# Two Swin blocks on one core: the bias of q and k moved from a matmul of its own into a constant channel of the normalised tile

## The reference, cut to what matters

```python
xn  = (x - mean(x)) * rsqrt(var(x) + 1e-5) * gamma + beta      # over the 192 channels
xs  = roll(xn, (-4, -4))                                       # windows of 8 x 8 = 64 tokens
qkv = xw @ w_qkv + b_qkv                                       # 192 -> 3 * 192, 12 heads of 16
...
x   = x + softmax(q @ k.T / 4 [+ bias + mask]) @ v @ w_proj + b_proj
x   = x + gelu(layernorm(x) @ w_fc1 + b_fc1) @ w_fc2 + b_fc2   # 192 -> 768 -> 192
```

## Time and profile before

| what | value |
|---|---|
| median of the runs, lowest, highest | 4314.11, 4303.97, 4317.73 us |
| the profiled execution, time and span | 4314.22 and 4312.3 us |
| TensorE clock granted, mean | 0.999 |
| PE matmul busy | 4027.5 us, 93% |
| PE weight load busy | 2912.2 us, 68% |
| VectorE (DVE) busy | 3364.9 us, 78% |
| ScalarE (ACT) busy | 2709.6 us, 63% |
| GpSimd (POOL) busy | 3062.7 us, 71% |
| DMA traffic | 420.50 MB, mean 98 GB/s |

### The profile page before, as it was taken

The page is one execution under the profiler, slowest core; times in us unless marked ns, Lnnn a source line. Parts: engine busy times, 40 slices in busy tenths (PEclk is TensorE's granted clock), DMA queues, the critical chain, the costliest instruction groups (busy, mean ns, idle before and its releaser), DMA issues. The chain is left out here.

```text
span 4312.3 us, 175439 instructions
## 1 busy us (share of the span) xinstructions
PE 4027.5 (93%) x66384; PEld 2912.2 (68%) x66384; DVE 3364.9 (78%) x9085; ACT 2709.6 (63%) x5921; POOL 3062.7 (71%) x6257
## 2 busy tenths in 40 slices
PE   4999999999999999999999999999999999999998
PEld 2666667667766666776676677667667766766665
DVE  6887777778778777787777778787777778777785
ACT  1666666666666666666666666666666666666665
POOL 4777777777777777777777777777777777777664
PEclk9999999999999999999999999999999999999999
DMA  4655556556565655555555555556555655565553
GB/s 98 104 96 100 98 95 99 102 95 99 104 98 97 100 102 92 103 100 96 98 100 98 97 99 102 97 97 101 102 91 101 100 97 98 100 101 96 90 95 61
DMA packets 1544449, 420.50 MB, mean 98 GB/s; under 512 B 1441334, under 2 KB 1542074, under 8 KB 1543612
## 3 DMA queue, kind: packets, MB, share of 16 engines
q1 hardware_dynamic: 1543612, 409.29, 54.9%
HBM read 31.56 MB, written 25.17 MB: 13 GB/s over the span
## 5 line engine op out<-in xcount | busy, mean ns | idle before, releaser
L573 PE MATMUL ps_s<-xh,w_fc 128*128 128x512 f16 x3840 | 909.7, 380 | 60.7 <-ACT stage L687 47.6
L941 DVE TENSOR_TENSOR hid<-scaled,hid 128x512 f16<-128x512 f32 x768 | 597.9, 779 | 449.7 <-POOL hid L1109 430.7
L1047 POOL TENSOR_TENSOR rstd<-vare,half 128x2 f32<-128x2 f32 x520 | 361.2, 695 | 801.5 <-DVE vare L881 801.5
L586 PE MATMUL bank<-w_fc,hid 128*128 128x192 f16 x9216 | 847.7, 246 | 77.7 <-DVE hid L941 71.9
L586 PEld LDWEIGHTS bank<-w_fc,hid 128*128 128x128 f16 x9216 | 764.6, 98 | 156.7 <-DVE v_blk L897 80.6
L573 PEld LDWEIGHTS ps_s<-xh,w_fc 128*128 128x128 f16 x3840 | 335.3, 97 | 621.0 <-ACT scaled L701 217.5
L1109 POOL TENSOR_SCALAR hid<-scaled 128x512 f16<-128x512 f32 x768 | 609.4, 794 | 182.8 <-ACT scaled L701 182.2
L701 ACT ACTIVATE scaled<-ps_s,b_fc 128x512 f32<-128x512 f32 x768 | 529.3, 690 | 308.9 <-DVE hid L941 306.8
L693 ACT ACTIVATE pt<-ps_t 128x768 f16<-128x768 f32 x512 | 415.3, 811 | 324.0 <-PE ps_t L530 316.8
L666 ACT ACTIVATE xs<-xn 128x192 f16<-128x192 f32 x512 | 184.6, 361 | 579.0 <-POOL xn L1053 579.0
L449 PE MATMUL bank<-w_qkv,xh 128*128 128x384 f16 x2560 | 500.9, 326 | 6.2 <-DMA xh<-xs 3.6
(11 more groups left out here) (113 smaller groups left out, 7341.9 us busy)
## 6 DMA issues: line engine op xcount, KB each, us to landing
x_img<-in_x_dram SPq DMA_DIRECT2D x256, 96.0 KB, 2.2
out_dram<-y_img SPq DMA_DIRECT2D x256, 96.0 KB, 1.9
xh<-xs SPq DMA_TRANSPOSE x520, 2.8
qkt<-qk SPq DMA_TRANSPOSE x512, 4.0
ot<-os SPq DMA_TRANSPOSE x512, 2.3
stage<-in_L_conv_fc_w_dram SPq DMA_DIRECT2D x2, 384.0 KB, 4.3
stage<-in_L_conv_w_fc_dram SPq DMA_DIRECT2D x2, 384.0 KB, 4.0
stage<-in_L_conv_qkv_w_dram SPq DMA_DIRECT2D x2, 288.0 KB
```

What stands on the lines that cost most here:

```text
L573: last = mm(ps_s[:, u % 2, :].rearrange("p (a t) -> p a t", a=GROUP), w_fc1[layer][:, part, m * 128:(m + 1) * 128], xh[:, p % 2 * GROUP:(p ...
L586: mm(bank[:, 0:C], hid16[:, hs, m, tok], w_fc2[layer][:, ws, m, :], start=(m == 0 and i == 0), stop=False)
L941: v.tensor_tensor(hid16[:, 1, m, :], hid[:, u % 2, :], hid16[:, 0, m, :], ALU.subtract)\
```

## The change

The bias matmul of `qk_product` goes. In its place the normalised tile's last channel (191) is the constant one in the high part and zero in the remainder, written once at the start. Since z sums to zero, z of channel 191 is minus the sum of the others; so the last weight row is subtracted from all rows (its own becomes zero), and that freed row of `w_qkv` gets the bias: its high part in the row of the high weights, its remainder in the row of the low weights. The columns of v keep a zero there.

In the steady state `normalise` for norm 1 and `norm1_lo` now write 191 channels. In the setup each layer gets two more loads before its first weight is ready (`w_last`, the last weight row on all 128 partitions, and `gain_last`), five more VectorE operations in `make_weight`, one copy less, and two small DMAs which write the bias into `w_qkv`, for which TensorE waits before the first slot. `rel` and `rel_t` are laid over `x_mid`, which is unused at that time.

```diff
-        b_qk = [sb(f"b_qk{l}", [128, 2 * C], F16) for l in range(LAYERS)]
+        qk_bias = sb("qk_bias", [1, LAYERS, 2, 2 * C], F16)
+        w_last = sb("w_last", [128, 3 * C], F32)
+        gain_last = sb("gain_last", [128, LAYERS], F32)
...
+                        last_row = L["wqkv"][C - 1:C, :]
+                        sp.dma_start(w_last[:, :], bass.AP(tensor=last_row.tensor, offset=last_row.offset,
+                                                           ap=[[0, 128], [1, 3 * C]])).then_inc(w_in[j], 16)
+                        last_gain = column(L["g1"], C - 1, 1)
+                        sp.dma_start(gain_last[:, l:l + 1], bass.AP(tensor=last_gain.tensor, offset=last_gain.offset,
+                                                                    ap=[[0, 128], [1, 1]])).then_inc(w_in[j], 16)
...
+                    if k == 3:
+                        for part in range(2):
+                            sp.dma_start(w_qkv[l][CB - 1:CB, 3 * part + 1, 0:2 * C], qk_bias[:, l, part, :])\
+                                .then_inc(bias_in, 16)
...
-        W_DMAS = [9, 4, 5, 1]
+        W_DMAS = [11, 4, 5, 1]
...
             pe.wait_ge(made, 1 + 4 * LAYERS)
+            pe.wait_ge(bias_in, 16 * 2 * LAYERS)
...
-                    contract(ps_qk[:, 0:2 * C], w_qkv[layer], xh[:, n % AHEAD, 0], 0, 2 * C, b_qk[layer][:, :])\
+                    contract(ps_qk[:, 0:2 * C], w_qkv[layer], xh[:, n % AHEAD, 0], 0, 2 * C)\
                         .then_inc(S["qk_mm"], 1)
...
-                v.memset(b_qk[l][:, :], 0.0)
...
+            v.memset(xs[:, :, 0, 0, C - 1:C].rearrange("p r c -> p (r c)"), 1.0)
+            v.memset(xs[:, :, 0, 1, C - 1:C].rearrange("p r c -> p (r c)"), 0.0)
...
+                if last is not None:
+                    for c0, c1, s in ((0, q_cols, WSCALE * QSCALE), (q_cols, n, WSCALE)):
+                        link(v.tensor_scalar(w_last[:, c0:c1], w_last[:, c0:c1], last, s, ALU.mult, ALU.mult))
+                    for rows in range(3):
+                        link(v.tensor_tensor(scaled[:, rows, 0:n], scaled[:, rows, 0:n], w_last[:, 0:n], ALU.subtract))
...
-                link(v.tensor_copy(row16[:, :], row[:, 0:2 * C]))
-                link(v.tensor_copy(b_qk[l][0:1, :], row16[:, :]))
-                link(v.tensor_tensor(b_qk[l][32:33, :], row[:, 0:2 * C], row16[:, :], ALU.subtract))
+                link(v.tensor_copy(qk_bias[:, l, 0, :], row[:, 0:2 * C]))
+                link(v.tensor_tensor(qk_bias[:, l, 1, :], row[:, 0:2 * C], qk_bias[:, l, 0, :], ALU.subtract))
...
-                    g_.tensor_scalar(dst, stream(n, which), nmean[:, r, which:which + 1], rstd[:, r, which:which + 1],
-                                     ALU.add, ALU.mult).then_inc(S[done], 1)
+                    m = dst.shape[-1]
+                    g_.tensor_scalar(dst, stream(n, which)[:, 0:m], nmean[:, r, which:which + 1],
+                                     rstd[:, r, which:which + 1], ALU.add, ALU.mult).then_inc(S[done], 1)
...
-                    normalise(n, 0, xs[:, n % 2, 0, 0, :], "hi1")
-                    normalise(n, 0, xn[:, 0, n % 2, :], "ln1")
+                    normalise(n, 0, xs[:, n % 2, 0, 0, 0:C - 1], "hi1")
+                    normalise(n, 0, xn[:, 0, n % 2, 0:C - 1], "ln1")
...
-                    g_.tensor_tensor(xs[:, n % 2, 0, 1, :], xn[:, 0, n % 2, :], xs[:, n % 2, 0, 0, :],
-                                     ALU.subtract).then_inc(S["lo1"], 1)
+                    g_.tensor_tensor(xs[:, n % 2, 0, 1, 0:C - 1], xn[:, 0, n % 2, 0:C - 1],
+                                     xs[:, n % 2, 0, 0, 0:C - 1], ALU.subtract).then_inc(S["lo1"], 1)
```

More of the change, by code:

```diff
@@ L162, in swin_program @@
         k_mask = sb("k_mask", [128, KINDS + 1, REGIONS], F32)
-        rel = sb("rel", [128, WIN, HEADS], F32)
-        rel_t = sb("rel_t", [128, 2, PAIRS, WIN], F32)
         bias_tab = sb("bias_tab", [128, 2, PAIRS, WIN], F16)
@@ L189, in swin_program @@
         x_mid = sb("x_mid", [128, TILES, C], F32)
+        rel = x_mid[:, 0:TILES // 2, :].rearrange("p t c -> p (t c)").rearrange("p (k h) -> p k h", h=HEADS)
+        rel_t = x_mid[:, TILES // 2:TILES, :].rearrange("p t c -> p (t c)")\
+            .rearrange("p (a g k) -> p a g k", a=2, g=PAIRS)
         x_tok = sb("x_tok", [128, 3 * TILES, C], F32)
@@ L218, in swin_program @@
         folded = sem("folded")
+        bias_in = sem("bias_in")
         made = sem("made")
@@ L798, in split, with make_weight @@
                 link(v.tensor_tensor(lo, src, hi, ALU.subtract))
-            def make_weight(w, place, n, gain, q_cols=0):
+            def make_weight(w, place, n, gain, q_cols=0, last=None):
                 for rows in range(3):
@@ L816, in _ @@
                 dve.wait_ge(w_in[4 * l], 16 * W_DMAS[0])
-                make_weight(w_qkv[l], 0, 3 * C, cols[:, l, 0, :], q_cols=C)
+                make_weight(w_qkv[l], 0, 3 * C, cols[:, l, 0, :], q_cols=C, last=gain_last[:, l:l + 1])
                 dve.wait_ge(folded, 3 * l + 1)
```

## The result

The changed kernel takes 4277.97 us (median of 6 runs, 4275.24 to 4286.51); the kernel before, run beside it, 4316.32 us (4303.97 to 4317.73). The ratio over all runs is 0.992 with a 95% interval of 0.9906 to 0.9934, 0.8% faster; the two medians lie 38 us apart. The profiled execution took 4277.42 us with a span of 4275.6 us, against 4312.3 us before: 36.7 us less, and this difference is what the traces have to account for.

What follows compares the result with a forecast made beforehand. Bound: per group, the hidden chain, TensorE's stream from place 1's `mlp_out` to place 0's `scores`, then VectorE and GpSimd. 4314.2 - 20.2 - 8.2 - 2.5 - 1.6 + 5.8 = 4287.5, forecast 4288 us, range 4270 to 4314.

Steps and rivals of the forecast that it cites:

- The regular part: Repeating groups of four slots: savings of 20.2, 8.2 and 2.5 us from the removed matmul at places 2 and 3.
- Places 0 and 1: Slots where TensorE waits anyway, for the Exp and for `hidden_lo(5)`: removing the matmul gains nothing.
- place 2: Slot where `mlp_out` follows the bias matmul without waiting: the whole 0.162 us counts, 20.2 us over 125 groups.
- place 3: Slot with two kinds of group: 0.13 us with layer 1's MLP (8.2 us), about 0.04 with layer 0's (2.5 us).
- all 83 us come out: Rival: every removed matmul's 0.162 us counts at all 512 tiles, time 4237 us; chance 0.02.
- VectorE takes the place: Rival: VectorE's chain through `o_norm` and `row_max` replaces TensorE's and limits the gain, 4305 to 4318 us; chance 0.26.
- weight load's share tells the distance to the roofline: Counterargument from the skill: at 68% TensorE would not be the bound, nothing gained, 4318 us; no separate chance.
- GpSimd's two-scalar operation at 191 columns is slower: Rival on `apply1` and `norm1_lo`: 0.07 us more each costs 26 us, all the gain; forecast counted 0; chance 0.08.
- the case that stood for 4260 to 4280: Between the forecast and the full gain: some unseen gain at places 0 and 1; more than forecast 0.10 in all.
- Setup, forecast +5.8: Before the first slot: extra DMAs and VectorE operations delay the first slot's matmul by 5.8 us, bounds 2.9 and 9.
- Layer 0: VectorE starts when `ident` lands: +1.0: Setup step: `ident` is issued behind two new DMAs at about 0.5 us each, so VectorE starts 1.0 us later.
- The fill, forecast -1.6: First seven tiles: 0.32 us saved on each of three at the lower clock, 0.16 on the next four, 1.6 in all.

Runs made afterwards that it cites:

- e5: Kernel before, with the bias matmul of q and k left out at places 0 and 1 only: 4311.7 us, ratio 0.9992.
- e6: Kernel before, with the bias matmul of q and k left out at place 2 only: 4289.0 us, ratio 0.9938.
- e7: Kernel before, with the bias matmul of q and k left out at place 3 only: 4298.6 us, ratio 0.9965.
- e8: Changed kernel with all 192 columns written again by norm 1 and `norm1_lo`, overwriting the constant channel: 4282.3 us.
- e10: Changed kernel with its setup reordered: `ident` and `vcol` load ahead of the two new loads, bias DMAs go after the last weight: 4277.1 us.
- e1: Kernel before with 288 unused bytes ahead of `xn`, putting the four tiles where the change has them: 4308.2 us, ratio 0.9989.
- e9: Kernel before with 32 unused bytes ahead of `xn`, so the four tiles start 256 bytes past a multiple of 512: 4306.6 us, ratio 0.9983.
- e3: Kernel before without the bias matmul of q and k anywhere, setup and addresses unchanged: 4276.1 us.
- e4: Kernel before without the bias matmul of q and k and with 288 unused bytes ahead of `xn`: 4272.4 us.
- e2: Changed kernel with 224 unused bytes ahead of `xn`, putting the four tiles back where the kernel before had them: 4284.5 us.
- e11: Changed kernel with 160 unused bytes ahead of `os`, so `os`, `ot` and `hid16` start at a multiple of 512: 4280.6 us.

## Why the prediction was right, and where its sum was off

**The regular part was right, and its mechanism held at each place.** Places 0 and 1 give nothing (e5), place 2 gives 0.17 us per group (forecast 0.162), place 3 gives 0.17 us in groups of layer 1's MLP (0.13) and 0.03 in those of layer 0's (0.04). Together the periods fell by 0.31 and 0.18 us (0.29 and 0.20). The distances from start to start of the earlier trace rows were the right measure, and the matmul's span of 327 ns was not: 512 of those would be 167 us.

By the Trainium skill ("TensorE: Matmul & The Clock Gate", section "Back-to-back issue gap") a matmul in a long stream would be worth an estimated 0.114 us; e6, where exactly one is taken out of the stream per group, gives 0.17, so the trace's 0.162 was the right price.

**The rivals.** That all 83 us come out fell with e5: half of them are waits now. That VectorE takes the place fell with e6 and e7: each period fell by the whole of what TensorE could give. The prediction had read the rule of the Trainium skill ("Trainium Kernel Development and Optimization", "Best Practices") that weight load's share tells the distance to the roofline so that nothing would come out at 68%; e6 alone gained 25 us, so that reading does not hold: the share is a mean over the span and doesn't say at which place TensorE is waited for. GpSimd's two-scalar operation at 191 columns is slower, by 9 to 16 ns, not by the 70 ns from which the gain would be gone; the estimate of nothing for it was near enough (e8).

**What was luck.** The gain in the profiled execution is 36.7 us, and a third of it, 12 us, comes from a term that the forecast did not have. Its range down to 4270 covered the result, but the case that stood for 4260 to 4280 was an unseen gain at places 0 and 1 (given 0.10 together with the full gain), and e5 shows none there. The direction and the size of the regular part were earned; that the time still fell in the range was not.

**Setup, forecast +5.8, measured +7.6.** The step "Layer 0: VectorE starts when `ident` lands: +1.0" was 1.7, as `ident` was issued 0.95 us later and landed another 0.7 us later. And the two bias DMAs were taken as costing nothing, since nobody waits long for them; but they are issued for 1.23 us at 33.69 on the SP queue, ahead of layer 1's columns. What is queued behind a DMA on its queue was what the step left out, not its own completion. VectorE's start on layer 1's weight came 4.4 us later, where 2.9 was forecast: the last load that it needs, `vcol`, was issued 3.6 us later (48.84 against 45.23), and VectorE waited for it until 52.17. Before, VectorE was busy with L845 until 47.75 and did not wait, so when `vcol` landed there was not in the rows, and "must just have landed" left out the other 0.8 us. e10 moves the bias DMAs and the new loads out of the way, and 3.2 us come back; it does not tell the two apart.

**The fill, forecast -1.6, measured -0.1.** The rows of the three first slots are nearer to each other, 3.40 us apart instead of 3.72 (`qk_product` starts at 90.25, 93.65 and 97.05 us), but by the first `hidden(0)` it was gone again. The fourth `qk_product` shows where, beside that of e10, which has the same fill:

```profile
102.88 1.81 PE L464 MATMUL bank<-w_qkv,xh 128*128 128x384 f16 x5
...
99.33 0.97 PE L466 MATMUL bank<-w_qkv,xh 128*128 128x384 f16 x5
```

In the changed kernel's execution the next matmul starts 1.60 us behind the first of these five, in e10's after 0.81: TensorE ran at half the rate for one tile more than in the kernel before, which costs about 1.3 us with what stands around it. Where the rate rose in time, the forecast holds: from the first slot's matmul to the first `hidden(0)` it is 64.5 us in e10 and 64.8 in e8, against 65.97 before, so 1.1 to 1.4 us are gained. (The profile's clock column reads 1.00 in all these stretches; that the first tiles run slower is seen only from start to start, 0.32 us for the bias matmul at 84.22 us and 0.16 later.)

**The term that was not in the sum: 12 us of irregular groups.** The prediction took the measured time apart into a regular pattern and changed that pattern. 24 us of the kernel before lie outside of it. In the 14 kernels of the table the excess follows the issue waits of PE closely, from 3.9 and 11.3 us to 15.5 and 24.0 us: about 1.2 us for each microsecond of issue wait, on top of some 6 us. Group by group it is the same, as the 16 and the 7 groups above show. So the excess beyond that floor is time in which TensorE stood without a reason that the profile shows, passed on to the end.

These waits are not strewn at random: e1 has the instructions of the kernel before and differs only in addresses, and of its 13 groups with an issue wait 9 are among the 16 of the kernel before, where chance would give about 2. In the 61st group both stop for 0.75 us in the same `mlp_out` (L586), then for 1.43 and 1.16 us before the same projection. So the waits hang at least in part on the spot in the program.

What lowers the excess is only partly found. With the bias matmul there, moving four tiles lowers it by 7 and 13 us (e1, e9) and the median by 5 and 6 us. Without the matmul it is low at either address (e3 11.7, e4 15.4, after 11.7, e2 10.3). The kernels that keep a part of the matmuls lie between (e5 20.9, e6 20.0, e7 17.0). The two causes don't add up, and builds that differ in nothing that should matter (after, e8, e10, e11) differ by up to 4 us. Each of these figures is one profiled execution, and the executions of one build differ by as much: those of e3 and e9 were the fastest of theirs, 5.7 and 4.7 us below the medians. What is shown is that moving the four tiles lowers the time (the intervals of e1 and e9 end below 1), with less excess in the trace. That leaving matmuls out lowers the excess too is likely (it is lower in e3, e5, e6 and e7 at the old addresses, and each median falls by 3 to 6 us more than the periods and, in e3, the fill give), but in none of them is that clear of its own interval. How either acts, and why TensorE's instructions come late there, stays open.

In sum, against the forecast's 4287.5 us for an execution like the profiled one: setup +1.8, fill +1.5, regular groups 0, excess -12, and the end -1.2 beyond the five periods that the forecast counted there. That gives the 4277.4 measured, within 0.2 us.

**The best version.** The changed kernel stands. Of the kernels that compute the whole reference, only e10 has a lower median, by 0.9 us, and the intervals (0.9897 to 0.9925, and 0.9906 to 0.9934) overlap. e3 and e4 are faster still, but leave the bias of q and k out.

## What to carry to other kernels

Price a removed instruction by the distance from start to start where it stands, once for every place where it occurs, and for each place name what starts the next instruction: where that is a wait for another engine, the saving turns into waiting (here 41 of 83 us). A regular pattern is not the whole time: sum what lies above it (here 24 us, 0.6%), and look there at waits for "issue", before a forecast claims a few tenths of a per cent. One profiled execution is not the median: place it among the runs before its excess is compared with another's. A change that allots other tiles also moves those behind them, so compare the DMA lines of the page, and try a start at a multiple of 256 bytes for the tiles that a DMA transpose reads or writes: it gave about 5 us here, for `xs`, `xh`, `qk` and `qkt`, and nothing for `os` and `ot`.

## What the runs showed of the hardware

- A DMA transpose depends on where its tiles start in a partition. With `xs`, `xh`, `qk` and `qkt` 224 bytes past a multiple of 512, the queue's share is 54.9 to 56.6%, `xh` lands after 2.8 us and `qkt` after 4.0; at 0 or 256 bytes past, 48.6 to 50.5%, 2.5 to 2.6 and 3.3 to 3.5 us; packets and bytes are the same in the kernel before, e1 and e9. The Trainium skill ("DMA: Bandwidth & Descriptors", section "How a descriptor splits into AXI transactions") has a possible reason, by the vendor's account: a descriptor that starts off a 256-byte boundary fetches the bytes below it too. The four tiles agree with it, though no run shows that this is what they pay for. `os` and `ot` don't: at 64, 96, 352 or 0 bytes past, `ot` lands after 2.3 us in all of them.
- GpSimd takes 514 to 517 ns for 191 columns of its two-scalar operation in the changed kernel, and 501 for 192 in e8 (504 in the kernel before). Its subtraction of two tiles (`norm1_lo`) doesn't show it: 549 ns for 191, 548 and 553 for 192.
- TensorE stands still within a stream of matmuls, with nothing in the profile that it waits for, for 0.2 to 2.1 us at a time, 6 to 22 times in an execution. Programs that differ by a tile nobody uses have 4.5 or 15.5 us of it, and many of the stops fall in the same groups (9 of e1's 13 are among the 16 of the kernel before).
- TensorE's rate rises at the start of the work by a step and not at a fixed tile: the fourth tile's five matmuls of q and k took 1.60 us from start to start in the changed kernel's execution and 0.81 in e10's.
